# Layer 0 of a two-layer graph network: sums kept by node, two source tiles accumulated in PSUM, self product in the first pair

## The chip, the cores and the metric

The kernel runs on one core of a Trainium2 chip. The core has a matmul engine (PE, with its weight loads shown apart as PEld), VectorE (DVE), ScalarE (ACT), GpSimd (POOL) and a queue engine for DMAs (SP). They run side by side and wait for one another by semaphores. The metric is the device time of one execution in microseconds, the median of several runs.

## The reference

x has 3125 nodes of 128 features; 103125 edges go src to dst, sorted by dst, with a weight each. `ln` is layer norm without scale.

```python
h = maximum(ln(x), 0)
# layer 0: edge_index = (src, dst); sums go to row = src, features come from col = dst
x = x + relu(h @ W_S.T + b_S + segment_sum((h[dst] @ W_N.T + b_N) * exp(-edge_weight)[:, None], src))
h = maximum(ln(x), 0)
# layer 1: attention over incoming edges
q, k, v = h @ Wq + bq, h @ Wk + bk, h @ Wv + bv
logits = sum(q[dst] * k[src]) / sqrt(128)
x = x + elu(segment_sum(softmax_by_dst(logits) * v[src]) + h @ Ws + bs)
```

## The kernel before

Nodes come in 25 tiles of 128 (NT, the last partly empty). The kernel turns the edge list into dense 128 x 128 blocks: for each tile of dst nodes it counts, per pair of nodes, the edges (for layer 1, as logarithms stored to memory) and sums the edge weights (for layer 0).

The stretch that matters is the loop over the 25 dst tiles (L1160, `pe_tile`). A tile has two quads of 64 nodes, each with four groups (`pe_group`). For a quad DVE builds tables from the edges (`quad`, L880): the key table (L895), the low table (L898) and three weighted copies (L901), 128 elements wide per edge slot. PE multiplies them into PSUM (L1144, L1146), ACT moves counts (L605, into gst) and weight sums (L607, into wst) out. DVE builds a quad's tables once PE is through with the quad two before.

Layer 0's sum for dst tile s then goes like this. wst holds the tile's weights [dst node, src node]. PE turns it (L1107, 25 transposes of 128 x 128 in seven pieces: six of four blocks and one of one block, the list `PC`) into PSUM; ACT copies each piece to wsb (L589), a buffer of two pieces. PE multiplies it (L1117): the stationary operand is hvb, a copy of the tile's neighbour features (L582), the moving one the piece of up to 512 columns, and the product, features by nodes, goes into a PSUM bank. DVE adds it into kT (L838), which holds the sum with features on partitions. So each dst tile takes 7 products and 7 adds over all 3125 nodes. PE does the products of a tile during the next tile, DVE the adds during the tile after that. What a slot of PE holds: two groups, then up to two products, then up to two pieces to turn.

The self product (L1094, seven matmuls with W_S stationary) fills kT before the loop proper, during tiles 0 and 1, and ACT adds the bias while it copies (L569).

After the loop kT is turned back to nodes on partitions, five blocks at a time (`turn_sums`, L1124), DVE applies relu, adds x (L850) and takes the statistics of the second layer norm (L854, L858). The five rounds of projections follow (POOL normalises, PE turns, ACT copies with relu to hc, PE multiplies for k, v, q and skip, L1241 and L1246), and turn_sums of round d + 2 stands in round d. k and q share a pair of PSUM banks. Then come 25 tiles of attention (scores L1278, values L1288), which the change does not touch.

Order on every engine is the order of the code; only semaphores tie the engines. All engines meet at the end of a stage (`end_stage`, L176).

## Time and profile before

| | us |
|---|---|
| runs, median (lowest, highest) | 849.43 (847.42, 849.62) |
| profiled execution, time | 856.0 |
| profiled execution, span | 854.2 |
| PE busy | 755.5 (88%) |
| PE weight loads busy | 655.8 (77%) |
| DVE busy | 740.0 (87%) |
| ACT busy | 505.8 (59%) |
| POOL busy | 263.3 (31%) |

The span is from the first to the last instruction of the profiled execution. A busy matmul row runs to its modelled end, about 0.16 us beyond the start of the next one, so paces are read from start to start. The first layer's loop stands between 62 and 474 us of the span, the projections to 515, attention behind it.

### The profile page before, as it was taken

The page shows a single profiled execution, that of the slowest core. Times are in us where ns is not written, and L with a number is a line of the kernel's source. Part 1 is how long each engine was busy: PE and PEld are TensorE (multiplying, and loading weights), DVE is VectorE, ACT ScalarE, POOL GpSimd, SP SyncE. Part 2 cuts the span into 40 slices and gives each one's busy share as a digit, 9 for nine tenths or more (in the row PEclk, how much of TensorE's full clock was granted, in tenths as well). Part 3 has the DMA queues.
Part 4 walks back from the last instruction along what each step waited for, and adds up shares of the span by engine and source line. Part 5 has one row for each costly group of instructions (what it writes and reads, how often), then busy time and mean ns, then how long its engine had stood idle before and what let it go on. Part 6 is the DMA issues. An engine that isn't in the chain of part 4 may idle for free.

```text
span 854.2 us, 22930 instructions
## 1 busy us (share of the span) xinstructions
PE 755.5 (88%) x8801; PEld 655.8 (77%) x8848; DVE 740.0 (87%) x888; ACT 505.8 (59%) x1013; POOL 263.3 (31%) x205
## 2 busy tenths in 40 slices
PE   0258999999999999999999687899999999999996
PEld 0146777777777777777775466799999999999996
DVE  6776799999999999999994537899999999999982
ACT  4859766767677667676775251445456455445534
POOL 4634000000000000000000320556766766766766
PEclk9999999999999999999999798899999999999998
DMA  9821112313213123122131612203433433432400
GB/s 252 264 78 79 79 79 105 125 77 135 95 77 153 77 95 135 77 125 105 77 153 79 254 56 77 77 13 149 160 105 134 160 123 116 160 137 105 157 7 11
DMA packets 17661, 96.63 MB, mean 113 GB/s; under 512 B 2610, under 2 KB 8860, under 8 KB 11100
## 3 DMA queue, kind: packets, MB, share of 16 engines
q1 hardware_dynamic: 14572, 90.02, 27.8%
q0 software_dynamic: 3056, 6.17, 2.6%
q8 instruction: 21, 0.34, 0.2%
q14 instruction: 12, 0.10, 0.0%
HBM read 51.55 MB, written 44.63 MB: 113 GB/s over the span
## 4 chain that ended last, share of the span: by engine, by line
PE 70%; DVE 12%; issue 10%; ACT 5%; another core or an unknown queue 1%; DMA 1%; DVEq 1%; POOL 0%; POOLq 0%; ACTq 0%; PEldq 0%; PEld 0%
PE bank L1278 17%; PE bank L1288 16%; PE bank L1117 14%; PE bank L1107 5%; PE bank L1146 5%; DVE oh_key L901 5%; PE bank L1144 5%; DVE kT L838 3%; PE bank L1275 2%; PE bank L1241 2%; ACT kT L543 1%; PE bank L1246 1%; PE bank L1084 1%; DVE mx L1029 1%
## 5 line engine op out<-in xcount | busy, mean ns | idle before, releaser
L481 POOL TENSOR_TENSOR sm<-sm,mbc 128x896 f32<-128x896 f32 (+1 forms) x100 | 186.2, 1892 | 77.5 <-ACT mbc L703 77.5
L1117 PE MATMUL bank<-wsb,hvb 128*128 128x512 f32 (+1 forms) x350 | 165.2, 578 | 13.7 <-DVE kT L838 12.4
L1278 PE MATMUL bank<-qT,kT 128*128 (+1 forms) x1250 | 168.0, 279 | 6.9 <-issue 4.3
L1144 PE MATMUL bank<-oh_key,oh_lo 128*128 128x100 bf16 x1600 | 170.4, 208 | 1.9 <-ACT wst L607 1.9
L1146 PE MATMUL bank<-oh_key,oh_lo 128*128 128x50 bf16 x3200 | 170.8, 187 | 0.0
L1278 PEld LDWEIGHTS bank<-qT,kT 128*128 128x128 f32 x1250 | 163.8, 196 | 5.0 <-DVEq L178 1.2
L1146 PEld LDWEIGHTS bank<-oh_key,oh_lo 128*128 128x128 bf16 x3200 | 163.7, 97 | 1.1
L1144 PEld LDWEIGHTS bank<-oh_key,oh_lo 128*128 128x128 bf16 x1600 | 155.8, 97 | 7.7 <-issue 5.5
L589 ACT COPY wsb<-bank 128x512 f32<-128x512 f32 (+1 forms) x175 | 88.0, 552 | 106.4 <-PE bank L1107 106.4
L1288 PE MATMUL bank<-vals,sm 128*128 128x129 f32 x1250 | 148.5, 276 | 0.0
L1029 DVE TENSOR_REDUCE mx<-sm 128x128 f32<-128x3200 f32 x25 | 146.2, 5846 | 0.9
L707 ACT ACTIVATE sm<-sm 128x896 f32<-128x896 f32 (+1 forms) x100 | 86.8, 868 | 101.3 <-POOL sm L481 101.3
L1288 PEld LDWEIGHTS bank<-vals,sm 128*128 128x128 f32 x1250 | 144.7, 193 | 0.0
L901 DVE TENSOR_TENSOR oh_key<-oh_key,xt 128x1600 bf16<-128x1600 bf16 x150 | 141.9, 1002 | 0.0
L605 ACT ACTIVATE gst<-bank,tiny_col 128x400 f32<-128x400 f32 x200 | 122.8, 614 | 15.4 <-PE bank L1146 11.9
L465 POOL MEMSET vals<- 128x25 f32 x1 | 0.1, 142 | 401.8 <-PEq L178 401.8
L838 DVE TENSOR_TENSOR kT<-kT,bank 128x512 f32<-128x512 f32 (+1 forms) x175 | 105.6, 626 | 13.6 <-PE bank L1117 11.5
L983 DVE TENSOR_TENSOR sm<-bank,gl_sb 128x896 f32<-128x896 f32 (+1 forms) x100 | 98.6, 986 | 21.2 <-PE bank L1278 20.2
L898 DVE TENSOR_TENSOR oh_lo<-xt,lo_tab 128x4096 bf16<-128x4096 bf16 x50 | 114.2, 2284 | 0.0
L1107 PEld LDWEIGHTS bank<-ident,wst 128*128 128x128 f32 x625 | 82.0, 193 | 30.7 <-issue 30.0
L1117 PEld LDWEIGHTS bank<-wsb,hvb 128*128 128x128 f32 x350 | 56.4, 189 | 59.3 <-DVE kT L838 33.1
L607 ACT COPY wst<-bank 128x400 f32<-128x400 f32 x200 | 101.3, 506 | 0.0
(123 smaller groups left out, 697.9 us busy)
## 6 DMA issues: line engine op xcount, KB each, us to landing
gt<-gst SPq DMA_DIRECT2D x25, 1600.0 KB, 5.6
gl_sb<-gt SPq DMA_DIRECT2D x25, 1600.0 KB, 6.7
records<-rec SPq DMA_DIRECT2D x1, 2015.0 KB
out<-res SPq DMA_DIRECT2D x24, 64.0 KB, 1.6
src_i<-in_src SPq DMA_DIRECT2D x1, 403.0 KB, 6.5
w_in<-in_edge_weight SPq DMA_DIRECT2D x1, 403.0 KB, 6.9
dst_i<-in_dst SPq DMA_DIRECT2D x1, 403.0 KB, 7.4
dstn_i<-in_dst_next SPq DMA_DIRECT2D x1, 403.0 KB, 7.3
```

What stands on the lines that cost most here:

```text
L481: pool.tensor_tensor(part, part, mbc[:, v % 2:v % 2 + 1, :].to_broadcast([P, n, P]), ALU.subtract).then_inc(sub_done, 1)
L605: nc.scalar.activation(place, counts, ACT.Ln, bias=tiny_col[:, 0:1], scale=EULER).then_inc(evacs, 1)
L838: V.tensor_tensor(kT[:, cols], kT[:, cols], ps(6 + at)[:, 0:n * P], ALU.add).then_inc(l0_add, 1)
L898: V.tensor_tensor(oh_lo[:, u, :, :, :], along(F_LO, P), table(lo_tab, P), ALU.is_equal).then_inc(onehot, 1)
L901: V.tensor_tensor(block(1 + w), block(0), along(F_W + w, KEYS), ALU.mult).then_inc(onehot, 1)
L1029: V.tensor_reduce(mx[:], sm[:, v, :].rearrange("p (h d) -> p d h", d=P), AX, ALU.max).then_inc(mx_ready, 1)
L1107: ins = T.transpose(ps(4 + at)[:, h * P:(h + 1) * P], tile, ident[:])
L1117: T.matmul(ps(6 + at)[:, 0:n], hvb[:, w, :], wsb[:, at, 0:n], start=True, stop=True).then_inc(l0_mm, 1)
L1144: T.matmul(cells, lo, oh_key[:, u, m, 0:2 * KEYS, i], start=True, stop=False, skip_group_check=True)
L1146: ins = T.matmul(cells[:, KEYS:2 * KEYS], lo, oh_key[:, u, m, (1 + w) * KEYS:(2 + w) * KEYS, i], start=False, stop=w == 2, skip_group_chec ...
L1278: ins = T.matmul(score_bank(g)[:, j * P:(j + 1) * P], kT[:, (a + j) * P:(a + j + 1) * P], qT[:, bass.ds(t * P, P)], start=g < LIFT, stop=T ...
L1288: ins = T.matmul(ps(4 + v % 2)[:, 0:D + 1], sm[:, v, h * P:(h + 1) * P], vals[:, h, :], start=h == 0, stop=h == NT - 1)
```

## The change

The stationary operand of layer 0's products becomes the turned weights, 128 nodes at a time, and the moving one the neighbour features hv of the tile (128 columns), so the sum stands with nodes on partitions. `pe_sum` accumulates two dst tiles (a pair, 2p and 2p + 1) in PSUM before DVE adds the piece to kT once (`add_sum`). For the first pair the self product is accumulated in the same place, and DVE adds the bias, now a row (brow), instead of adding to kT. Both tiles' turned weights must be kept whole: wsb is now qT (free in this stage) for even tiles and wsb1 for odd ones. The copy hvb, the self products ahead of the loop, `turn_sums` and their semaphores are gone. Three tables say in which slot of a tile pieces are turned (TURNS), summed (SUMS) and added (ADDS, early and late place of each quad). Each table's first row is for even tiles, the second for odd ones. q's projection gets the bank pair that turn_sums used.

```diff
+
+
+TURNS = (((0, 1, 2), (3, 4), (5, 6), ()), ((0, 1), (2, 3), (4,), (5, 6)))
+SUMS = ((None, 0, 1, 2), (3, 4, 5, 6))
+ADDS = (((4, 5), (6, None)), ((0, 1), (2, 3)))
...
-        wsb = sb(s2, "wsb", [P, 2, 4 * P])
-        hvb = sb(s2, "hvb", [P, 2, D])
-        past_gl = sb(s2, "past_gl", [P, (P + KEYS) * (QN - TWO)], BF16)
+        wsb1 = sb(s2, "wsb1", [P, NP])
+        wsb = (qT, wsb1)
...
-            for i, b in enumerate((b_s, bq, bk)):
+            for i, b in enumerate((bq, bk)):
                 sp.dma_start(bcol[:, i:i + 1], b.rearrange("(p a) -> p a", a=1)).then_inc(s_wts, 16)
-            for i, b in enumerate((b_n, bv, b_skip)):
+            for i, b in enumerate((b_n, bv, b_skip, b_s)):
                 sp.dma_start(brow[:, i, :], b.rearrange("(a f) -> a f", a=1).to_broadcast([P, D])).then_inc(s_wts, 16)
...
-            def act_hv(s, w):
-
-                act.wait_ge(l0_mm, NPC * s + 1)
-                nc.scalar.copy(hvb[:, w, :], hv[:, bass.ds(s, 1), :].rearrange("p t f -> p (t f)")).then_inc(hvb_ready, 1)
-
-            def act_piece(s, w, j):
-                n = PC[j][1] * P
+            def act_piece(s, w, j, q):
+
+                a, n = PC[j][0], PC[j][1] * P
                 at = (w + j) % 2
                 act.wait_ge(turned, NPC + 1 + NPC * s + j + 1)
-                act.wait_ge(l0_mm, NPC * s + j + 1)
-                nc.scalar.copy(wsb[:, at, 0:n], ps(4 + at)[:, 0:n]).then_inc(l0_ev, 1)
+                act.wait_ge(l0_mm, NPC * (q + 1) + j + 1)
+                nc.scalar.copy(wsb[w][:, a * P:a * P + n], ps(4 + at)[:, 0:n]).then_inc(l0_ev, 1)
...
-                        if isinstance(t, int) and t == 1 and j == 1:
-                            act_self(4, NPC)
-                            act.wait_ge(s_hvb, len(TG))
-                        if before and j == 1:
-                            act_hv(t - 1, 1 - v)
-                        if before and j % 2 == 1:
-                            for piece in range(j - 1, min(j + 1, NPC)):
-                                act_piece(t - 1, 1 - v, piece)
+                        if p is not None and j % 2 == 1:
+                            for piece in TURNS[v][j // 2]:
+                                act_piece(t - 1, 1 - v, piece, p)
...
-                nc.scalar.activation(kT[:, cols], pair(2)[:, 0:CW], ACT.Identity, bias=bcol[:, 2:3]).then_inc(proj_a, 1)
+                nc.scalar.activation(kT[:, cols], pair(2)[:, 0:CW], ACT.Identity, bias=bcol[:, 1:2]).then_inc(proj_a, 1)
                 act.wait_ge(q_mm, d + 1)
-                nc.scalar.activation(qT[:, cols], pair(2)[:, 0:CW], ACT.Identity, bias=bcol[:, 3:4],
+                nc.scalar.activation(qT[:, cols], pair(0)[:, 0:CW], ACT.Identity, bias=bcol[:, 2:3],
                                      scale=float(D) ** -0.5).then_inc(proj_a, 1)
...
-            def dve_piece(s, w, j):
+            def add_sum(q, j, first=False):
 
                 a, n = PC[j]
-                at = (w + j) % 2
-                dve.wait_ge(l0_mm, 2 + NPC * s + j + 1)
-                dve.wait_ge(l0_add, NPC * s + j + 3)
-                cols = slice(a * P, (a + n) * P)
-                V.tensor_tensor(kT[:, cols], kT[:, cols], ps(6 + at)[:, 0:n * P], ALU.add).then_inc(l0_add, 1)
+                dve.wait_ge(l0_mm, 2 * NPC + NPC * q + j + 1)
+                part, rows = ps(6 + j % 2)[:, 0:n * P], kt3[:, a:a + n, :]
+                if first:
+                    V.tensor_tensor(rows, part.rearrange("p (t f) -> p t f", f=D),
+                                    brow[:, 3:4, :].to_broadcast([P, n, D]), ALU.add).then_inc(l0_add, 1)
+                else:
+                    dve.wait_ge(l0_add, 3 + NPC * q + j)
+                    flat = kT[:, a * P:(a + n) * P]
+                    V.tensor_tensor(flat, flat, part, ALU.add).then_inc(l0_add, 1)
...
-                dve.wait_ge(r_turned, d + 1)
-                V.scalar_tensor_tensor(out=flat, in0=pair(0)[:, 0:CW], scalar=0.0, in1=flat, op0=ALU.max,
+                V.scalar_tensor_tensor(out=flat, in0=kT[:, d * CW:(d + 1) * CW], scalar=0.0, in1=flat, op0=ALU.max,
...
                 for j in range(NPC):
-                    dve_piece(NT - 1, 0, j)
-                    if j == 2:
+                    add_sum(q, j)
+                    if j == 3:
+                        dve.wait_ge(l0_add, NPC + 2 + NPC * q + 2)
                         statistics(0)
...
+                    early, late = ADDS[v][u] if p is not None else (None, None)
+                    if early is not None:
+                        add_sum(p, early, first)
                     V.tensor_tensor(oh_lo[:, u, :, :, :], along(F_LO, P), table(lo_tab, P), ALU.is_equal).then_inc(onehot, 1)
+                    if late is not None:
+                        add_sum(p, late, first)
                     dve.wait_ge(onehot, (t * 2 + u) * HOTS + 1)
                     for w in range(3):
                         V.tensor_tensor(block(1 + w), block(0), along(F_W + w, KEYS), ALU.mult).then_inc(onehot, 1)
-                    for j in later:
-                        dve_piece(t - 2, v, j)
...
-                with dve.Fori(1, NT // 2) as i:
-                    dve_tile(i * 2, 0, True)
-                    dve_tile(i * 2 + 1, 1, True)
-                dve_tile(NT - 1, 0, True)
+                dve_tile(2, 0, None)
+                dve_tile(3, 1, 0, first=True)
+                dve_tile(4, 0, 0, first=True)
+                dve_tile(5, 1, 1)
+                with dve.Fori(3, NT // 2) as i:
+                    dve_tile(i * 2, 0, i - 2)
+                    dve_tile(i * 2 + 1, 1, i - 1)
+                dve_tile(NT - 1, 0, NT // 2 - 2)
                 for j in range(NPC):
-                    dve_piece(NT - 2, 1, j)
-                dve_last_tile()
+                    add_sum(NT // 2 - 1, j)
+                dve_last_tile(NT // 2)
...
-            def pe_self(from_, to):
-                pe.wait_ge(s_hnev, len(TG))
-                for j in range(from_, to):
-                    a, k = PC[j]
-                    if j >= 2:
-                        pe.wait_ge(acc_ev, j - 1)
-                    T.matmul(ps(6 + j % 2)[:, 0:k * P], wts[:, WS_, :], hT[:, a * P:(a + k) * P], start=True,
-                             stop=True).then_inc(acc_mm, 1)
...
-            def pe_product(s, w, j):
-                n = PC[j][1] * P
-                at = (w + j) % 2
-                if j == 0:
-                    pe.wait_ge(hvb_ready, s + 1)
-                pe.wait_ge(l0_ev, 2 + NPC * s + j + 1)
-                pe.wait_ge(l0_add, NPC + NPC * s + j + 1)
-                T.matmul(ps(6 + at)[:, 0:n], hvb[:, w, :], wsb[:, at, 0:n], start=True, stop=True).then_inc(l0_mm, 1)
-
-            def turn_sums(d):
-                if d >= 1:
-                    pe.wait_ge(ln_step, d * 3 - 2)
-                for j in range(HC):
-                    a = (d * HC + j) * P
-                    ins = T.transpose(pair(0)[:, j * P:(j + 1) * P], kT[:, a:a + P], ident[:])
-                ins.then_inc(r_turned, 1)
-
-            def pe_last(j):
-
-                if j == 4:
-                    pe.wait_ge(l0_add, NPC + 2 + NPC * (NT - 1) + 2)
-                    turn_sums(0)
+            def pe_sum(q, j, parts, first=False):
+
+                a, k = PC[j]
+                if first and j == 0:
+                    pe.wait_ge(s_hnev, len(TG))
+                    pe.wait_ge(s_hvb, len(TG))
+                pe.wait_ge(l0_add, NPC + 2 + NPC * q + max(j - 1, 0))
+                for s, w in parts:
+                    pe.wait_ge(l0_ev, 2 + NPC * s + j + 1)
+                for h in range(k):
+                    cols = slice((a + h) * P, (a + h + 1) * P)
+                    to = ps(6 + j % 2)[:, h * P:(h + 1) * P]
+                    if first:
+                        T.matmul(to, hT[:, cols], wts[:, WS_, :], start=True, stop=False, skip_group_check=True)
+                    for n, (s, w) in enumerate(parts):
+                        ins = T.matmul(to, wsb[w][:, cols], hv[:, bass.ds(s, 1), :].rearrange("p t f -> p (t f)"),
+                                       start=n == 0 and not first, stop=n == len(parts) - 1, skip_group_check=True)
+                ins.then_inc(l0_mm, 1)
...
                         if isinstance(t, int) and t == 0 and j == 6:
-                            pe_self(0, 4)
                             turn_windows(3, 5)
                         if isinstance(t, int) and t == 1 and j == 0:
-                            pe_self(4, NPC)
-                            pe.wait_ge(acc_ev, NPC)
                             pe.wait_ge(s_xtev, NB)
-                        if two_before and j == 0:
-                            pe_products(t - 2, v, SLOTS0)
+                        if p is not None and SUMS[v][j // 2] is not None:
+                            pe_pair(p, SUMS[v][j // 2], first)
                         if before:
-                            pe_products(t - 1, 1 - v, j)
-                            pe_turns(t - 1, 1 - v, j)
+                            pe_turns(t - 1, 1 - v, TURNS[v][j // 2])
...
-                pe_tile(0, 0, False, False)
-                pe_tile(1, 1, True, False)
-                with pe.Fori(1, NT // 2) as i:
-                    pe_tile(i * 2, 0, True, True)
-                    pe_tile(i * 2 + 1, 1, True, True)
-                pe_tile(NT - 1, 0, True, True)
-                pe_products(NT - 2, 1, SLOTS0)
-                for j in range(0, SLOTS0 + 2, 2):
-                    pe_products(NT - 1, 0, j)
-                    pe_turns(NT - 1, 0, j)
-                    pe_last(j)
+                pe_tile(0, 0, None, before=False)
+                pe_tile(1, 1, None)
+                pe_tile(2, 0, 0, first=True)
+                pe_tile(3, 1, 0, first=True)
+                with pe.Fori(2, NT // 2) as i:
+                    pe_tile(i * 2, 0, i - 1)
+                    pe_tile(i * 2 + 1, 1, i - 1)
+                pe_tile(NT - 1, 0, NT // 2 - 1)
+                for d in range(NG):
+                    pe_pair(NT // 2 - 1, SUMS[1][d])
+                    pe_turns(NT - 1, 0, TURNS[1][d])
+                for j in range(NPC):
+                    pe_sum(NT // 2, j, [(NT - 1, 0)])
...
-                if d + 2 < NC:
-                    turn_sums(d + 2)
                 pe.wait_ge(hc_ready, d + 1)
                 if d >= 1:
                     pe.wait_ge(proj_a, d * 2)
                     pe.wait_ge(proj_v, d * 2)
                 across(2, WK_, k_mm)
                 down(3, WV_, v_mm)
-                pe.wait_ge(proj_a, d * 2 + 1)
-                across(2, WQ_, q_mm)
+                across(0, WQ_, q_mm)
                 pe.wait_ge(proj_v, d * 2 + 1)
                 down(3, WX_, skip_mm)
```

On PE, in the loop, behind the two groups of the third slot of an even tile; hvb and wsb are the features and turned weights before, hv and qT or wsb1 those after. Before:

```order
L1115 REGISTER_ALU
L1116 REGISTER_ALU
L1117 MATMUL bank3<-wsb,hvb 128x512
L1115 REGISTER_ALU
L1116 REGISTER_ALU
L1117 MATMUL bank3<-wsb,hvb 128x512
L1107 MATMUL bank2<-ident,wst1 128x128 x8
```

After:

```order
L1102 REGISTER_ALU x2
L1109 MATMUL bank3<-hv,qT 128x128
L1109 MATMUL bank3<-hv,wsb1 128x128
L1109 MATMUL bank3<-hv,qT 128x128
L1109 MATMUL bank3<-hv,wsb1 128x128
L1109 MATMUL bank3<-hv,qT 128x128
L1109 MATMUL bank3<-hv,wsb1 128x128
L1109 MATMUL bank3<-hv,qT 128x128
L1109 MATMUL bank3<-hv,wsb1 128x128
L1085 REGISTER_ALU
L1091 MATMUL bank2<-ident,wst1 128x128 x4
```

Two wide products and two turned pieces stood in the slot. Now it holds one piece of a pair: eight matmuls of 128 columns, each with another stationary operand, and then the turned pieces.

On DVE, in the loop, the first quad of an even tile: the key table, the adds into kT, the low table. Before:

```order
L895 TENSOR_TENSOR oh_key<-xt,key_tab 128x16x100
L835 ISA
L838 TENSOR_TENSOR kT<-kT,bank3 128x512
L835 REGISTER_ALU
L838 TENSOR_TENSOR kT<-kT,bank3 128x512
L898 ISA
L898 TENSOR_TENSOR oh_lo<-xt,lo_tab 128x4096
```

After:

```order
L883 TENSOR_TENSOR oh_key<-xt,key_tab 128x16x100
L818 ISA
L824 REGISTER_ALU
L826 TENSOR_TENSOR kT<-kT,bank3 128x512
L887 ISA
L887 TENSOR_TENSOR oh_lo<-xt,lo_tab 128x4096
L818 REGISTER_ALU
L824 REGISTER_ALU
L826 TENSOR_TENSOR kT<-kT,bank3 128x512
```

Two adds stood between the two tables. Now there is one, and a second stands behind the low table, ahead of the weighted copies.

On ACT, in the loop, behind the first two groups of an even tile (the copies of turned pieces out of bank2). Before:

```order
L587 REGISTER_ALU
L589 COPY wsb<-bank2 128x512
L587 REGISTER_ALU
L588 REGISTER_ALU
L589 COPY wsb<-bank2 128x512
```

After:

```order
L580 REGISTER_ALU
L582 COPY wsb1<-bank2 128x512
L580 REGISTER_ALU
L582 COPY wsb1<-bank2 128x512
L580 REGISTER_ALU
L582 COPY wsb1<-bank2 128x512
```

Two pieces were copied there, now three.

## Rows read from the trace of the kernel before

**Rows 1.** Windows view, one tile of the first layer (busy us per engine, PEclk, DMA)
```profile
250.85:266.43 15.58, 15.14 (x237) 11.87 (x233) 15.50 (x18) 10.91 (x25) 0.00 (x0) 1.00 0.25 105
```

**Rows 2.** Timeline of PE, the tile from 257.04 (start us, us, engine, line)
```profile
257.04 0.21 PE L1144 MATMUL bank<-oh_key,oh_lo 128*128 128x100 bf16 x1
...
258.63 0.47 PE L1117 MATMUL bank<-wsb,hvb 128*128 128x128 f32 x2
...
262.97 1.13 PE L1117 MATMUL bank<-wsb,hvb 128*128 128x512 f32 x2 [0.44 <-DVE kT L838]
263.94 1.06 PE L1107 MATMUL bank<-ident,wst 128*128 128x128 f32 x8
...
266.43 1.96 PE L1117 MATMUL bank<-wsb,hvb 128*128 128x512 f32 x4
...
272.62 0.21 PE L1144 MATMUL bank<-oh_key,oh_lo 128*128 128x100 bf16 x1
```

**Rows 3.** Timeline of DVE in the same tile
```profile
262.83 0.99 DVE L895 TENSOR_TENSOR oh_key<-xt,key_tab 128x1600 bf16<-128x1600 bf16 x1
263.74 1.28 DVE L838 TENSOR_TENSOR kT<-kT,bank 128x512 f32<-128x512 f32 x2
264.93 2.29 DVE L898 TENSOR_TENSOR oh_lo<-xt,lo_tab 128x4096 bf16<-128x4096 bf16 x1
267.13 2.79 DVE L901 TENSOR_TENSOR oh_key<-oh_key,xt 128x1600 bf16<-128x1600 bf16 x3
269.84 1.28 DVE L838 TENSOR_TENSOR kT<-kT,bank 128x512 f32<-128x512 f32 x2
```

**Rows 4.** Timeline of ACT in the same tile
```profile
260.90 0.65 ACT L605 ACTIVATE gst<-bank,tiny_col 128x400 f32<-128x400 f32 x1
261.39 0.54 ACT L607 COPY wst<-bank 128x400 f32<-128x400 f32 x1
261.77 0.66 ACT L605 ACTIVATE gst<-bank,tiny_col 128x400 f32<-128x400 f32 x1
...
264.66 1.07 ACT L589 COPY wsb<-bank 128x512 f32<-128x512 f32 x2 [1.84 <-PE bank L1107]
```

**Rows 5.** Chain of waits in the attention layer (start us, us, what)
```profile
600.43 2.90 PE bank L1288 x26
```

**Rows 6.** Timeline of PE at the same place
```profile
603.17 2.83 PE L1278 MATMUL bank<-qT,kT 128*128 x22
```

**Rows 7.** Timeline of PE, first tiles, from three windows
```profile
76.73 3.87 PE L1094 MATMUL bank<-hT,wts 128*128 128x512 f32 x8
...
83.52 0.21 PE L1144 MATMUL bank<-oh_key,oh_lo 128*128 128x100 bf16 x1
...
101.20 0.21 PE L1144 MATMUL bank<-oh_key,oh_lo 128*128 128x100 bf16 x1
```

**Rows 8.** Timeline of DVE, the third tile's first table
```profile
91.04 0.99 DVE L895 TENSOR_TENSOR oh_key<-xt,key_tab 128x1600 bf16<-128x1600 bf16 x1 [8.21 <-PE bank L1146]
```

**Rows 9.** Timeline of PE: the last tile's first group, a late product
```profile
444.04 0.21 PE L1144 MATMUL bank<-oh_key,oh_lo 128*128 128x100 bf16 x1
...
471.59 1.10 PE L1117 MATMUL bank<-wsb,hvb 128*128 128x512 f32 x2 [2.30 <-DVE kT L838]
```

**Rows 10.** Timeline of DVE at the end of the first layer
```profile
468.47 0.82 DVE L850 SCALAR_TENSOR_TENSOR xs<-bank,xs 128x640 f32<-128x640 f32 x1 [1.61 <-PE bank L1124]
...
473.68 0.29 DVE L838 TENSOR_TENSOR kT<-kT,bank 128x128 f32<-128x128 f32 x1 [0.27 <-PE bank L1117]
```

**Rows 11.** Windows view, at the start of the projections
```profile
480.20:482.40 2.20, 2.13 (x10) 2.00 (x10) 0.85 (x8) 1.00 (x2) 0.85 (x2) 0.50 1.06 448
```

**Rows 12.** Chain of waits in the projections
```profile
482.67 1.89 PE bank L1241 x4
...
485.67 1.11 PE bank L1241 x4
```

**Rows 13.** Timeline of PE, second round of the projections
```profile
489.31 1.35 PE L1241 MATMUL bank<-hc,wts 128*128 128x512 f32 x4 [0.25 <-ACT hc L684]
```

More of the change, by code:

```diff
@@ L954, in _ @@
                     next_numbers(f_dnum, FD)
-                with dve.Fori(0, NT // 2) as i:
-                    for w in range(2):
-                        for j in range(NPC):
-                            dve_piece(i * 2 + w, w, j)
-                dve_last_tile()
+                for j in range(NPC):
+                    add_sum(0, j, first=True)
+                with dve.Fori(1, NT - 1) as s:
+                    for j in range(NPC):
+                        add_sum(s, j)
+                dve_last_tile(NT - 1)
             end_stage(dve, 2)
-            V.tensor_scalar(bcol[:, 3:4], bcol[:, 1:2], float(D) ** -0.5, None, ALU.mult).then_inc(s_qb, 1)
+            V.tensor_scalar(bcol[:, 2:3], bcol[:, 0:1], float(D) ** -0.5, None, ALU.mult).then_inc(s_qb, 1)
             inverse(0)
@@ L1148, in pe_group, with pe_pair, pe_turns, pe_tile @@
                     ins.then_inc(groups, 1)
-                def pe_products(s, w, j):
-                    for piece in range(max(j - 2, 0), min(j, NPC)):
-                        pe_product(s, w, piece)
-                def pe_turns(s, w, j):
-                    if j == 0:
-                        pe.wait_ge(evacs, 4 + (s + 1) * 2 * SLOTS0)
-                    for piece in range(j, min(j + 2, NPC)):
-                        pe_turn(s, w, piece, True)
-                def pe_tile(t, v, before, two_before):
+                def pe_pair(p, j, first=False):
+                    pe_sum(p, j, [(p * 2, 0), (p * 2 + 1, 1)], first)
+                def pe_turns(s, w, pieces):
+                    for j in pieces:
+                        if j == 0:
+                            pe.wait_ge(evacs, 4 + (s + 1) * 2 * SLOTS0)
+                        pe_turn(s, w, j, True)
+                def pe_tile(t, v, p, before=True, first=False):
                     for j in range(0, SLOTS0, 2):
@@ L1219, in _, with pe_tile_slow @@
                         pe.drain().then_inc(fs_mm, 1)
-                def pe_tile_slow(s, w, uses, last=False):
+                def pe_tile_slow(s, w, uses, first=False):
                     pe.wait_ge(fs_wl[w], uses * 16 + 16)
```

72 lines of the change are left out of this document (29 added, 43 removed).

## The prediction

> **What bounds the kernel now.** I read the page first (busy shares, chain), then the windows of the first layer, then one tile of it engine by engine in the timeline. The change touches only that layer and the projections behind it. In one tile of 15.58 us PE is busy 15.14 and DVE 15.50, at full granted clock [rows 1]; ACT has room. The reader is to see that two engines are full at once, and to ask which of them really works. PE's tile runs from 257.04 to 272.62 [rows 2]. Two groups of count matmuls take 1.59 (257.04 to 258.63), four such pairs a tile: 6.4. Eight transposes take 0.9 (the 1.06 of the row holds the last one's end), so 25 take 2.8. Two products of 512 columns take 1.80 (1.96 less the end), so the tile's 6.25 take 5.6 to 5.7. Sum 14.9; the remaining 0.7 is waiting, 0.44 of it for a DVE add into kT in the row at 262.97. DVE [rows 3]: key table 0.91 (262.83 to 263.74), two adds 1.19, low table 2.20, three weightings 2.71. Twice the tables is 11.6, seven adds (six full at 0.60, one of 0.19) are 3.8: 15.4 of 15.58. So DVE bounds the tile, and PE is only 0.7 behind it. That is the most that relieving DVE can give, per tile.
>
> **DVE.** Adds go from seven per tile to seven per two tiles: 175 become 91. DVE's work falls to 11.6 + 1.9 = 13.5 per tile. None of that shows by itself beyond PE's 14.9.
>
> **PE in the loop.** Per tile 7 products with 7 weights (512 columns) become 25 products with 25 weights (128 columns). The trace has the same form in the attention layer: fp32, new weights for each, 26 records in 2.90 [rows 5], 0.1117 us a record, two records per product (one of those streams 129 columns). 25 x 2 x 0.1117 = 5.6 per tile, what the wide ones took. So PE's work per pair of tiles is 12.8 groups + 5.6 transposes + 11.2 sums = 29.5, and 0.1 for the starts of pieces. The bound on the other side is the neighbouring row, 22 records in 2.83 [rows 6], 0.129 each, end and a halt between groups included. I take 0.1117 since the sums stand 16 records in a row with no halt inside.
>
> **New waits in the loop.** (1) In an even tile three pieces are turned in one go behind the first two groups, with two PSUM buffers. The third needs ACT's copy of the first. Count from the groups' start: groups end 1.59; ACT begins on the second group about 0.25 later (ACT takes up a turned piece at 264.66, where the first four of the transposes from 263.94 are issued by 264.39 [rows 2, 4]), and its two moves take 0.49 and 0.38 (260.90, 261.39, 261.77 [rows 4]), but the first group's moves hold it, so it is free at 2.8. Copy 0.54 and 0.12 to pass it on: 3.45. PE has done two pieces at 2.49. It waits 0.96. (2) DVE's fifth piece. Count from the end of the even tile's fourth group: PE runs sum 0, turn, two groups, sum 1, turn and so on, and ends sum 5 at 21.9, the pair's last turn at 24.9. DVE may add piece 5 only then: 22.14 to 22.74, the three weightings to 25.45, and PE starts the next even tile at 25.57 instead of 24.93: 0.64. The waits that DVE itself gets (1.5 for piece 1, 1.5 for piece 5) lie in its spare time otherwise. Pair: 29.6 + 0.96 + 0.64 = 31.2, against 2 x 15.58 = 31.16. Ten pairs: **+0.5**. The loop changes its bound, not its length.
>
> **Start.** The self product was 3.7 (76.73 to 80.43, from the row's 3.87) and 3.0 more behind tile 1's first groups. It goes, so tile 1 begins at 79.8 instead of 83.52 [rows 7]. Tile 1 then needs 6.4 + 2.8 of PE and 1.1 of waits, ending at 90.1. DVE's table for tile 2 can start once tile 1's first four groups are done (two pairs of groups and a turn between, 1.59 + 0.90 + 1.59) and 0.25 passed, at 84.1 instead of 91.04 [rows 8]; with 5.8 of tables and no adds tile 2 starts at 90.1 instead of 101.20: -11.1. But tiles 2 and 3 now carry the self products too: 25 x 2 x 0.1117 = 5.6 on 29.5, with 1.3 of waits 36.4 against 31.16: +5.2. **Start: -5.9.**
>
> **End.** Before, from the last tile's first group (444.04 [rows 9]) to the last add (473.68 + 0.29 [rows 10]) 29.9. After, PE lags further: the last tile (6.4 groups, 5.4 sums, 2.8 transposes, 0.96 wait) 15.5, then sums 3 to 6 of the pair 5.8, transposes 2.8, the single tile's sums 5.6, about 2.0 for an add standing behind the statistics (the same wait is 2.30 now [rows 9], where the statistics begin at 468.47 [rows 10]), the last add 0.5: 32.2. **End: +2.3.**
>
> **Projections.** Five transposes per round (turn_sums) go, and q gets a bank of its own. The rounds do not shorten: the key product waits for ACT's relu copy, which hangs on the transpose before, not on turn_sums (wait of 0.25 left at 489.31 [rows 13]), and each copy out of the shared bank is over when v's product ends. What may be lost is clock: PE is at 0.50, the lower level of 1.2 GHz, with 10 records of transposes under way [rows 11], and its first key product takes 1.89 where a later one takes 1.11 [rows 12]. Without turn_sums PE does less before the rise. Bounds: nothing, or v and q of the first round at half clock too, 2 x 1.1 = +2.2. I take **+1.0**, between.
> The Trainium skill (TensorE: Matmul & The Clock Gate, Part 4: PE-mode transpose) says that a transpose does not count as PE activity for the clock as other matmuls do. By that, taking transposes away delays nothing, and this term is 0; by the row alone it stays open.
>
> **Sum.** -5.9 + 0.5 + 2.3 + 1.0 = -2.1. The profiled execution took 856.0 (span 854.2), the median shown is 849.43; the change of 2.1 on either gives 853.9 and **847.3**. Nothing in the attention layer moves.
>
> **Rivals.**
> A (forecast): loop bound moves from DVE to PE at equal length; 847.3, own range 843 to 851.
> B, faster: the two new waits don't arise or half close, because ACT and DVE pass work on sooner than my 0.25 and 0.12. For it: each depends on under 1 us. Against: the copy stands behind four moves of ACT whatever the latency. Price: 1.6 x 12 = 19 if both go (828), the DVE one alone 0.64 x 12 = 8: 840.
> C, slower: short fp32 products with their own weights, register addresses and three semaphore checks per piece don't reach 0.1117. Place: each sum piece on PE. 1250 records in the layer, so each ns costs 1.25 us; from 0.1155 a record the kernel is slower by over 0.3%. At 0.120, half way to rows 6, +10.4: 858; at 0.129 +21.6: 868. For it: rows 6; against: rows 5, and the same layer's transposes at 0.113.
> D, slower: the jump back at PE's loop end costs a fetch, since its body grows by 72 matmul records and their weight loads. Before, tile 272.62 starts without a gap [rows 2]. If 3 us came at each of 10 rounds: 877.
> For D the Trainium skill (Runtime: NRT & Kernel Launch, Instruction fetch mechanics) says that PE's instruction store holds 2048 instructions and that a jump out of the held part stalls; by that number both bodies fit, and D adds 0.
> That the change does not do what it says (adds not halved) has no room: the count of adds is fixed by the code.
>
> **Chances.** A 0.48, B 0.25, C 0.24, D 0.03. A change of 0.3% (2.5 us) is about what can be told from none. A splits 0.40 faster, 0.50 same, 0.10 slower; B nearly all faster; C mostly slower, 0.20 of it same. Faster 0.19 + 0.24 = 0.43, same 0.24 + 0.01 + 0.06 = 0.31, slower 0.05 + 0.18 + 0.03 = 0.26. The range reaches to B's nearer price and to C's nearer one: 839 to 858.
>
> **What would show it.** DVE's busy share in the loop falls to about 13.5 of 15.6, PE's stays near 15; a pair of tiles lasts 31.2; 16 records of a sum take 1.79 to 1.82; the third turned piece waits 0.96 for ACT and the even tile's first group 0.64 for DVE's weighting; tile 2 starts near 90, tile 4 near 126.5; the layer ends near 471 instead of 474. A pair under 30.5 or sums over 1.85 would prove it wrong, and so would a gap at the loop's jump.

## The result and the profile after

The changed kernel took 854.18 us (median; 852.44 to 855.72), the kernel before 849.43 in the same comparison: 1.0051 times as long, 95% interval 1.0033 to 1.0068, that is +4.2 to +4.8. In a second comparison the same two kernels stood at 860.39 and 856.16: 1.0049 [1.0029, 1.0068]. The forecast was 847.3, 0.25% faster. The time lies in the range of 839 to 858, but the sign is wrong.

The level moved by 6.7 us from one comparison to the next for the kernel before itself. A row shows where such a step can come from: ahead of the layer, the profiled execution of before holds for 6.56 us (41.24, "another core or an unknown queue" in its chain), the one of after doesn't, and the repetition of after has 7.17 at 40.36. So kernels are compared here by their ratio to the kernel before in the same comparison, and traces from the layer's first group of count matmuls on.

The page of the changed kernel, profiled execution (span 852.8, 854.67 in all):

```profile
PE 760.9 (89%) x9759; PEld 735.2 (86%) x9759; DVE 698.9 (82%) x804; ACT 498.9 (59%) x981; POOL 267.2 (31%) x205
...
PE 78%; DVE 8%; ACT 6%; issue 5%; DMA 1%; POOL 0%; DVEq 0%; PEld 0%; ACTq 0%; POOLq 0%; PEldq 0%
```

DVE's 740.0 became 698.9, as wanted, but PE rose from 755.5 to 760.9 and its share of the chain from 70% to 78%. The bound has moved to PE.

Timeline of PE after the change: the first groups of tiles 1, 2 and 4, then the pair of tiles from 249.00, then the last tile (start us, us, engine, line; in brackets the wait ahead and who ended it). It answers to [rows 2, 7, 9]:

```profile
74.38 0.21 PE L1124 MATMUL bank<-oh_key,oh_lo 128*128 128x100 bf16 x1
84.78 0.22 PE L1124 MATMUL bank<-oh_key,oh_lo 128*128 128x100 bf16 x1 [0.32 <-DVE oh_key L892]
121.91 0.22 PE L1124 MATMUL bank<-oh_key,oh_lo 128*128 128x100 bf16 x1 [0.23 <-DVE oh_key L892]
...
249.00 0.22 PE L1124 MATMUL bank<-oh_key,oh_lo 128*128 128x100 bf16 x1 [0.54 <-DVE oh_key L892]
250.61 1.15 PE L1091 MATMUL bank<-ident,wst 128*128 128x128 f32 x8
252.41 0.72 PE L1091 MATMUL bank<-ident,wst 128*128 128x128 f32 x4 [0.65 <-ACT wsb L582]
254.56 0.47 PE L1109 MATMUL bank<-hv,qT 128*128 x2
254.86 0.39 PE L1109 MATMUL bank<-hv,wsb 128*128 x2
264.78 0.21 PE L1124 MATMUL bank<-oh_key,oh_lo 128*128 128x100 bf16 x1
280.78 0.22 PE L1124 MATMUL bank<-oh_key,oh_lo 128*128 128x100 bf16 x1 [0.54 <-DVE oh_key L892]
...
439.46 0.22 PE L1124 MATMUL bank<-oh_key,oh_lo 128*128 128x100 bf16 x1 [0.37 <-DVE oh_key L892]
```

A pair of tiles lasts 280.78 - 249.00 = 31.78, over all ten (439.46 - 121.91) / 10 = 31.75; before it was 31.17. Both forecast waits are there and in their places: the third turned piece waits for ACT, the even tile's first group for DVE's weighting. From the starts of the rows around them the second costs 0.71. In the first PE stands still for 0.82, and the first transpose behind it takes 0.10 more than the others, 0.9 together.

The pair of rows at 254.56 and 254.86 holds what the forecast lacks. Each has two records, but the second begins 0.30 after the first, and from then on one follows the other each 0.22 (2 x 0.1117): the first fp32 product behind the bf16 groups costs 0.08 more. So a sum of 16 records takes 1.87. In the tail of the layer the same kernel has a sum that stands behind transposes, and it takes 1.78, from 457.91 to 459.69:

```profile
457.91 0.39 PE L1109 MATMUL bank<-hv,qT 128*128 128x128 f32 x2
...
459.69 1.06 PE L1091 MATMUL bank<-ident,wst 128*128 128x128 f32 x8
```

The rows of weight loads (PEld) show what goes with it. The load of a sum's first record starts 0.03 ahead of its product (254.53, 254.56), that of the third 0.11 ahead (254.75, 254.86). Behind the wait for ACT load and transpose start together (252.41):

```profile
252.41 0.41 PEld L1091 LDWEIGHTS bank<-ident,wst 128*128 128x128 f32 x3 [0.84 <-ACT wsb L582]
...
254.53 0.30 PEld L1109 LDWEIGHTS bank<-hv,qT 128*128 128x128 f32 x2
254.75 0.30 PEld L1109 LDWEIGHTS bank<-hv,wsb 128*128 128x128 f32 x2
```

The lead that is missing, 0.08 and 0.11, is about the extra, 0.08 and 0.10. So the fp32 weight load that nothing covers may be the cause, rather than the change of type. No run separates the two.

DVE at the end of the layer, and PE's wait there, answering to [rows 9, 10]:

```profile
468.45 0.82 DVE L837 SCALAR_TENSOR_TENSOR xs<-kT,xs 128x640 f32<-128x640 f32 x1
...
470.76 1.52 DVE L826 TENSOR_TENSOR kT<-kT,bank 128x512 f32<-128x512 f32 x3
```

```profile
471.47 0.49 PE L1109 MATMUL bank<-hv,qT 128*128 128x128 f32 x2 [1.73 <-DVE kT L826]
```

The last sum waits 1.73 for an add that stands behind the statistics, and the last add ends at 472.28.

Where the time went, stage by stage. The second pair of traces is the repetition of both kernels:

| stage | forecast | first pair of traces | second pair |
|---|---|---|---|
| start: first group to tile 4 | -5.9 | 66.96 - 70.14 = -3.2 | 66.96 - 70.11 = -3.2 |
| ten pairs of tiles | +0.5 | 317.55 - 311.67 = +5.9 | 317.49 - 311.67 = +5.8 |
| end: last tile to last add | +2.3 | 32.82 - 29.93 = +2.9 | 32.83 - 30.25 = +2.6 |
| projections | +1.0 | 43.31 - 41.50 = +1.8 | 43.46 - 40.60 = +2.9 |
| sum of these | -2.1 | +7.4 | +8.1 |
| attention to the end | 0 | -1.5 | -1.2 |
| ahead of the first group | 0 | -7.3 (the hold) | -0.8 |

The spans differ by the last three rows together, -1.4 and +6.1. The medians say +4.2 to +4.8; each trace is one execution, and the second pair comes from two comparisons. The attention's 1.2 to 1.5 is not laid to the change: the same attention code took 335.7 to 339.3 us in the traces of all kernels here. The loop alone is as large as the whole loss.

### The profile page after: what moved, and what is told of

It reads as the page before. It is cut to its first block, busy times and chain, and to the rows that moved or that the text cites. A ratio compares the mean times of both kernels' runs of the same rounds, so it can differ in the third digit from the quotient of the medians.

```text
span 852.8 us, 24429 instructions
## 1 busy us (share of the span) xinstructions
PE 760.9 (89%) x9759; PEld 735.2 (86%) x9759; DVE 698.9 (82%) x804; ACT 498.9 (59%) x981; POOL 267.2 (31%) x205
## 4 chain that ended last, share of the span: by engine, by line
PE 78%; DVE 8%; ACT 6%; issue 5%; DMA 1%; POOL 0%; DVEq 0%; PEld 0%; ACTq 0%; POOLq 0%; PEldq 0%
PE bank L1109 16%; PE bank L1259 16%; PE bank L1249 16%; PE bank L1126 8%; PE bank L1124 7%; PE bank L1091 6%; DVE oh_key L892 3%; PE bank L1246 3%; PE bank L1215 2%; PE bank L1220 1%; ACT kT L547 1%; PE bank L1077 1%; ACT wsb L582 1%; DVE mx L1022 1%; DVE junk L732 1%
## 5 line engine op out<-in xcount | busy, mean ns | idle before, releaser
L598 ACT ACTIVATE gst<-bank,tiny_col 128x400 f32<-128x400 f32 x200 | 121.0, 605 | 37.8 <-PE bank L1126 32.4
L1109 PE MATMUL bank<-hv,qT 128*128 (+1 forms) x650 | 128.3, 285 | 1.7 <-DVE kT L826 1.7
L1109 PE MATMUL bank<-hv,wsb 128*128 (+1 forms) x600 | 116.0, 275 | 0.0
L826 DVE TENSOR_TENSOR kT<-kT,bank 128x512 f32<-128x512 f32 (+1 forms) x84 | 52.7, 628 | 58.2 <-PE bank L1109 57.7
L600 ACT COPY wst<-bank 128x400 f32<-128x400 f32 x200 | 99.3, 496 | 0.0
L1109 PEld LDWEIGHTS bank<-hv,qT 128*128 128x128 f32 x650 | 96.7, 191 | 2.1 <-DVE kT L826 1.9
L1091 PE MATMUL bank<-ident,wst 128*128 128x128 f32 x625 | 88.8, 279 | 7.9 <-ACT wsb L582 7.9
```

Of the source, the lines that this page charges most:

```text
L598: nc.scalar.activation(place, counts, ACT.Ln, bias=tiny_col[:, 0:1], scale=EULER).then_inc(evacs, 1)
L600: nc.scalar.copy(sums, cells[:, :, KEYS:2 * KEYS]).then_inc(evacs, 1)
L1091: ins = T.transpose(ps(4 + at)[:, h * P:(h + 1) * P], tile, ident[:])
L1109: ins = T.matmul(to, wsb[w][:, cols], hv[:, bass.ds(s, 1), :].rearrange("p t f -> p (t f)"), start=n == 0 and not first, stop=n == len(par ...
```

## The experiments

**The two waits.** Only the tables of orders are edited. The first kernel changes TURNS, the second ADDS, the third both.

```
-TURNS = (((0, 1, 2), (3, 4), (5, 6), ()), ((0, 1), (2, 3), (4,), (5, 6)))
+TURNS = (((0, 1), (2, 3), (4, 5), (6,)), ((0, 1), (2, 3), (4,), (5, 6)))     first, third
-ADDS = (((4, 5), (6, None)), ((0, 1), (2, 3)))
+ADDS = (((4, None), (5, 6)), ((0, 1), (2, 3)))                               second, third
```

Turns alone: 

> The even tile turns two, two, two and one piece behind its four pairs of groups, not three, two, two and none. Theory (the pair of tiles lost 0.6 us to two waits and to 8 switches from bf16 groups to fp32 products at 0.08 us each, and each wait is worth its own length): the wait of the third turned piece for ACT (0.82 of a pair's 31.78) goes, PE is at work in its place, ten pairs of the loop fall by about 8 us, the first and last tiles by 1.5: 844.5 against 854.2. The sums stay at 1.865 us for 16 records and the wait for DVE's weighting at 0.7 a pair. Rival (the loop is held by something else, such as DVE's chain over the adds): the wait moves to another piece and the time stays within 1 us of 854.2.

Adds alone: 

> DVE adds pieces 5 and 6 of the pair in the even tile's second half, piece 4 in its first, so that no add stands between PE's sum 5 and the weighting of the next even tile. Theory: the wait of the even tile's first group for DVE's weighting (0.71 a pair) goes, 0.6 to 0.7 a pair, about 6 to 7 us in the loop: 847.5. Rival (the weighting is late because DVE itself is behind, or PE's sums then wait for the later adds to free their PSUM bank): a wait of the same size shows at a sum's first record, and the time stays at 854.

Both: 

> Both edits of the two kernels above. Theory (the waits are separate and add up): 1.5 a pair, a pair of 30.3, about 16 to 17 us in all: 837.5. What is left of a pair is 12.8 of groups, 11.7 of sums, 5.8 of transposes. Rival (one cover for the other: when one wait goes, the other grows): no better than the better of the two alone, 844 to 847.

Measured against before: turns 0.9917 [0.9893, 0.994], adds 0.9954 [0.9933, 0.9976], both 0.9825 [0.9801, 0.9848]. The changed kernel stands at 1.0049 in its repetition, so the edits are worth 1.3%, 0.9% and 2.2% (11, 8 and 19 us). The expected times were on the level of the first comparison; as shares of the changed kernel's time they were 0.989, 0.992 and 0.980, and 0.987, 0.991 and 0.978 came out. The pairs of tiles lasted 30.85, 31.05 and 30.15: less by 0.90, 0.71 and 1.61, and 0.90 + 0.71 is 1.61. The theory holds and both gains add up; the rivals (a wait that moves elsewhere, one wait that covers for the other) are excluded. PE in the kernel with both orders, a pair of tiles from 247.97 to 278.12, with no wait ahead of any first group, and the window of this pair (columns as in [rows 1]), where PE is busy all 30.15:

```profile
247.97 0.21 PE L1124 MATMUL bank<-oh_key,oh_lo 128*128 128x100 bf16 x1
...
262.83 0.21 PE L1124 MATMUL bank<-oh_key,oh_lo 128*128 128x100 bf16 x1
...
278.12 0.21 PE L1124 MATMUL bank<-oh_key,oh_lo 128*128 128x100 bf16 x1
```

```profile
247.97:278.12 30.15, 30.15 (x537) 30.06 (x535) 27.48 (x28) 21.59 (x47) 0.00 (x0) 1.00 0.26 109
```

**Wide products, tiles still paired.** hv becomes the weights again, and 512 columns of the turned sums stream. With it come back ACT's copy of hv into a fixed buffer, the bias by partition, and the transposes of the sums in the projections.

```
-                for h in range(k):                      # 128 columns, own weights each
-                        ins = T.matmul(to, wsb[w][:, cols], hv[:, bass.ds(s, 1), :]...)
+                cols = slice(a * P, (a + k) * P)        # up to 512 columns
+                    ins = T.matmul(to, hvb[:, w, :], wsb[w][:, cols], ...)
+                            act_hv(p, t - 2, 0, 2)      # in ACT's even tile, behind group 2
```

> Only the accumulation of two tiles in PSUM is kept; the products turn back to the wide form (hv of the tile as weights, 512 columns of the turned sums moving, features on the partitions), with the copy of hv by ACT, the bias by partition and the transposes of the sums ahead of the statistics. Orders and waits in the loop stay as after the change. Theory (the narrow form costs 0.8937 per 512 columns at 0.1117 a record where the wide one costs 0.86 at 0.43 a record, and both pay 0.08 when they follow bf16 groups): a sum falls from 1.865 to 1.80, 0.4 a pair, 4 to 5 us in the layer, and the projections' clock comes back with the transposes (1.5): about 848.5. The two waits stay at 0.7 to 0.8. Rival (the forecast's pricing: narrow and wide cost the same, the loss is in the waits alone): a sum at 1.86 in both, only the clock's 1.5 comes back: 852.5. Rival (the narrow form is the whole loss, as 25 weight loads per tile are not hidden): the pair of tiles falls below 31.0, total below 846.

It took 1.0128 [1.0106, 1.0149], slower than both kernels, which no expectation had. The pair lasted 32.41. One row says why, and it is a fault of the experiment: the copy of hv stood too late on ACT, and the first sum of each pair waited for it.

```profile
264.50 1.12 PE L1121 MATMUL bank<-qT,hvb 128*128 128x512 f32 x2 [0.87 <-ACT hvb L590]
```

Counted from the starts of the rows, the wait costs 1.05. Less that, the pair is 31.36, 0.39 under the changed kernel, and the sum itself is the 1.80 expected. A sum of 1.86 or a pair under 31.0, as the two rivals had it, did not come. A second version has both forecast waits removed and the copy ahead of the even tile's first evacuation:

> The wide form again, with both orders changed, and with ACT's copy of hv ahead of the even tile's first evacuation (the first wide kernel made PE wait 0.87 a pair for it). Theory: a sum 1.80 instead of 1.865 and the last one as before, 0.39 a pair less than the version with both orders (30.15): 29.8; start -0.5, projections' clock -1.5: 6 us under it, ratio 0.9755. Rival (the copy of hv by ACT and the longer records bring other waits of the same size): pair 30.1, ratio 0.981.

It took 0.9759 [0.9738, 0.978], pair 29.74, 0.41 under the 30.15 of the narrow form: both as expected. That the total fits is partly luck. Against the trace of the version with both orders the projections gave 0.4 instead of 1.5, and 1.6 came from tile 0, where the clock did not fall (see the start below). Two sums of it on PE, 256.79 to 258.60 and 260.29 to 262.10:

```profile
256.79 1.10 PE L1121 MATMUL bank<-qT,hvb 128*128 128x512 f32 x2
257.73 1.02 PE L1121 MATMUL bank<-wsb,hvb 128*128 128x512 f32 x2
...
260.29 1.10 PE L1121 MATMUL bank<-qT,hvb 128*128 128x512 f32 x2
261.23 1.02 PE L1121 MATMUL bank<-wsb,hvb 128*128 128x512 f32 x2
```

So the narrow form costs 0.4 a pair, 4 us in the loop, and the two waits 1.61. Two tiles per addition with the wide form are worth 31.17 - 29.74 = 1.43 a pair against the kernel before. By its ratio this is the fastest version that was run: 2.4% under the kernel before, 2.9% under the change.

**The price of going from bf16 to fp32.** Two kernels on the version with both orders. In the one the turned pieces stand between a slot's two groups (in the loop only), in the other ahead of its sum.

```
                         pe_group(t, j)
+                        if before and not isinstance(t, int): pe_turns(...)    # split
                         pe_group(t, j + 1)
+                        if before: pe_turns(t - 1, 1 - v, TURNS[v][j // 2])    # order: ahead of the sum
                         if p is not None and SUMS[v][j // 2] is not None: pe_pair(...)
-                        if before: pe_turns(t - 1, 1 - v, TURNS[v][j // 2])
```

Split: 

> On the version with both orders changed (pair 30.15): in the loop the turned pieces stand between the two groups of a slot, the sum behind the second, so PE goes 8 more times a pair from bf16 groups to fp32 records (one of the sum-less slot is there already: 7 more). Theory (each such turn of form costs 0.08 us, wherever it stands): 0.56 a pair more, 30.7, about +6 us of the total over the 0.9825 ratio: 0.989. Sums stay at 1.865. Rival (the 0.08 belongs to the sum's own start: its register address and three waits): transposes behind a group cost no more than behind a sum, the pair stays at 30.15, ratio 0.982.

Order: 

> On the version with both orders changed: the turned pieces of a slot stand ahead of its sum. The number of changes from bf16 to fp32 stays. Theory (the cost is of the first fp32 record behind bf16 groups): 16 records of a sum fall from 1.865 to 1.785 where pieces are turned ahead of them, the first transpose takes 0.19 instead of 0.11, the pair stays at 30.15 within 0.15. Rival (cost of the sum's own start): sums stay at 1.865, transposes at 0.1125.

Split took 1.0079 [1.0048, 1.0109], pair 32.29, far more than the 30.7 expected. Its PE rows show two things. New waits of the pieces for ACT, in the even tile, make up some 1.3 of the 2.1 a pair:

```profile
255.12 1.17 PE L1091 MATMUL bank<-ident,wst 128*128 128x128 f32 x8 [0.23 <-ACT qT L582]
258.65 1.21 PE L1091 MATMUL bank<-ident,wst 128*128 128x128 f32 x8 [0.75 <-ACT wsb L582]
```

And in the odd tile, which has none (270.61 to 286.26, 15.65 against 15.29), four more turns of form cost 0.36, 0.09 each. The size per turn was about right (0.08 expected), the total missed what the split does to ACT. Order took 0.9864 [0.9838, 0.989], pair 30.48. The row of its eight transposes behind groups, and the first two of the sum behind them:

```profile
252.01 1.15 PE L1091 MATMUL bank<-ident,wst 128*128 128x128 f32 x8
252.99 0.39 PE L1109 MATMUL bank<-hv,qT 128*128 x2
253.22 0.39 PE L1109 MATMUL bank<-hv,wsb 128*128 x2
254.78 0.21 PE L1124 MATMUL bank<-oh_key,oh_lo 128*128 128x100 bf16 x1
```

The sum is 254.78 - 252.99 = 1.79 instead of 1.865 and its first product has lost the extra, while the eight transposes ahead take 0.98 instead of 0.90 (254.00 to 254.90 in the version with both orders). The extra goes with the place behind the groups, not with the sum's address or its waits: that rival is excluded. Here the kernel was not within 0.15 of its base but 0.33 slower a pair, 0.26 of it a wait ahead of the odd tile's first group (the sum ends at 262.72, the group starts at 262.98), for which the trace names no releaser.

**Repetitions.** The changed kernel and the kernel before, each with a trace of its own:

> The changed kernel once more, beside the kernel before on this chip, since the kernel before took 856.2 in the last comparison and 849.4 in the first. Theory (the layer's loop alone is worth +5.9, the whole +4 to +5, whatever the level of the chip or of a start that waits longer for the windows): ratio 1.004 to 1.007, a pair of tiles of 31.75 to 31.78. Rival (part of the 0.5% was the one hold of 6.6 us ahead of the layer, present in one kernel and not in the other): ratio off by up to 0.008 either way with the same pair.

> The kernel before once more with a profile, for three readings that rest on one trace of it: the hold of 6.56 us ahead of the layer, the place at which the clock rises in the first projection round (v 1.28 there, 1.5 to 2.3 in the kernels after), and the 21 halts of 0.2 us in the attention layer's score matmuls, which no trace of the changed kernels shows. Theory for the clock (it scatters in the same code): v's ten records at 1.5 or more here too. Rival (the stage before has the earlier rise): 1.28 again. Halts: if they come again they belong to the kernel before and are worth 1.5 us to the change; if not, they were that one execution's. The pair of tiles stays at 31.17, ratio 1.000 within its interval.

The changed kernel came out at 1.0049 with a pair of 31.75, so the loss doesn't hang on the hold, which this trace has. The kernel before has the hold again (6.83 at 40.87) and gave 0.9981 [0.9961, 1.0001] against itself, pair 31.17. The halts of 0.2 us in the attention layer are absent (1.0 us of idle ahead of L1278 instead of 6.9), so they were of one execution. The rise of the clock came early again, v 1.28: the theory that it merely scatters failed, the rival held.

**The clock in the projections.** On the version with both orders:

```
+            def idle_turns():
+                for j in range(HC):
+                    T.transpose(pair(0)[:, CW:CW + P], wts[:, WS_, :], ident[:])
```

> The version with both orders changed, a second time, as the base that the two kernels of this comparison are read against and for the place in the first projection round at which the clock rises in a second trace. Ratio 0.980 to 0.985, pair 30.15; the clock rises in v's products (1.7 to 1.8 instead of 1.28) or as late as q's: the traces so far show 1.73 to 2.34 for v in the same code.

> On the version with both orders changed: five transposes whose result nothing reads stand at three places where the transposes of the sums stood before the change (behind the last tile's fourth sum, ahead of the first projection round, and behind that round's transposes of xn). Theory (PE's work ahead of the projections, transposes included, brings the rise of the clock forward, as the forecast's middle value had it): v's ten records at 1.28 to 1.5, q's four at 1.25, 0.5 to 1.5 us less, ratio 0.979 to 0.982. Rival (transposes do not bring the rise forward; what the traces show is scatter): v at 1.7 to 2.3 again, ratio within 0.001 of the base or up to 1 us more for the transposes themselves.

The ratio was 0.983 [0.9788, 0.9872] with the idle transposes, 0.9824 [0.9782, 0.9866] without. v's ten records took 1.48 with them, 1.54 and 1.73 in the two traces without (1.7 or more was expected of the second one, which gave 1.54). The 1.48 lies in the theory's range, the time in the rival's, and 1.48 against 1.54 is less than the scatter of the same code. So no effect of the transposes is seen, in one trace of them. That agrees with the forecast's other reading, by the Trainium skill (TensorE: Matmul & The Clock Gate, Part 4: PE-mode transpose): a transpose does not count as PE activity for the clock as other matmuls do. The two wide versions, which have the transposes of the sums again, point the same way: v took 1.50 and 1.78. But the kernel before rises earlier in both its traces, so something else of its stage matters. Its first round in the repetition:

```profile
481.43 1.72 PE L1241 MATMUL bank<-hc,wts 128*128 128x512 f32 x4
482.99 1.28 PE L1246 MATMUL bank<-wts,hc 128*128 128x128 f32 x10
484.11 1.28 PE L1241 MATMUL bank<-hc,wts 128*128 128x512 f32 x4
```

and the same three products (k, v, q) after the change:

```profile
481.18 2.50 PE L1215 MATMUL bank<-hc,wts 128*128 128x512 f32 x4 [0.85 <-ACT hc L668]
483.47 2.34 PE L1220 MATMUL bank<-wts,hc 128*128 128x128 f32 x10
485.60 1.45 PE L1215 MATMUL bank<-hc,wts 128*128 128x512 f32 x4
```

The granted clock is 0.50 until about 486 after the change; in the kernel before it rises inside k. Counted from the layer's last add, it rises after 8.8 and 10.1 us in the kernel before, and after 11.4 to 15.4 in the twelve traces of the changed kernel and its variants. There v took 1.48 to 1.78 in six and 2.34 in six, never 1.28, with or without transposes.

**The self product.** Left out of the version with both orders, so its output lacks x times W_s:

```
-                    if first:
-                        T.matmul(to, hT[:, cols], wts[:, WS_, :], start=True, stop=False, ...)
```

> On the version with both orders changed: the self product (x times W_s) is left out, 25 fp32 products of two records in tiles 2 and 3. Theory (they cost their 5.6 us one for one, since PE bounds these tiles): tile 2 to tile 4 takes 30.3 to 30.7 instead of 35.75, 5.0 to 5.4 us less, ratio 0.976 to 0.9765. Rival (DVE's tables bound tiles 2 and 3, which are still filling): 33 or more, ratio 0.980.

It took 0.9778 [0.9736, 0.9821]. From tile 2 to tile 4 it is 30.16 instead of 35.75: 5.6, one for one. The theory holds and the rival (DVE bounds these tiles) doesn't. But the total fell by less, 0.46% or 3.9 us. In the trace, against its base, tile 0 is 1.5 shorter, and the projections are 3.3 and the attention 3.3 longer. Of the projections 1.7 are a round in which the clock dropped once more:

```profile
471.50:473.50 2.00, 1.45 (x2) 0.68 (x3) 1.51 (x10) 0.49 (x1) 1.92 (x2) 0.69 0.03 8
473.50:475.50 2.00, 2.00 (x10) 1.75 (x9) 0.00 (x0) 0.79 (x1) 0.43 (x1) 0.50 0.00 0
```

(windows: length, busy PE, PEld, DVE, ACT, POOL, granted clock, DMA share, GB/s). The split version has such a round too (7.76 long like this one, 6.10 in the other traces), so it does not come from leaving the self product out.

## Why the prediction was wrong

**The bound and the rivals' mechanisms.** "The loop changes its bound, not its length" was right in its first half. DVE's relief does not show by itself, and both new waits are there (1.61 a pair, forecast 1.60), so rival B fails. There is no gap at the loop's jump (rival D): with both orders changed every pair starts without a wait.

**The step that failed: in "PE in the loop" the term "0.1 for the starts of pieces", where the runs show 8 x 0.08 = 0.64 a pair.** The pace was right, 0.1117 inside a sum. What was left out is the first product behind the groups, in 7 of the 8 slots of a pair, and the first transpose in the eighth. The wide products of before were priced with it: 1.80 for four records holds it once (4 x 0.43 + 0.08). The narrow ones, "what the wide ones took", were priced without. By measured terms the pair is 12.74 groups + 11.17 products + 5.59 transposes + 8 x 0.08 + 1.61 waits = 31.75, and without the waits 30.14, which is the 30.15 of the version with both orders. The forecast's 31.2 lacks 0.55, all of it in these starts. (Its own terms 12.8 + 5.6 + 11.2 make 29.6, not 29.5; by the measured terms 29.5 is right.)

The number stood in the rows that were used: in [rows 2] the two narrow records at 258.63, behind the groups, take 0.47, where the eight transposes take 1.06, of which 0.90 is eight paces and 0.16 the end. Two paces and that end are 0.39; 0.08 is left over.

In the kernel before, PE had 29.76 of work a pair and stood waiting for 1.40; after, 30.14 and 1.61. The ten pairs make the +5.9 measured against +0.5: 3.8 of work, which the narrow form brought, and 2.1 of waits.

**Rival C** named the right place, the sums, with the wrong cause. 1.865 for 16 records is 0.1166 each, above its point of decision at 0.1155, yet no record is slow except the first. The forecast's own sign of being wrong, "sums over 1.85", came. (In the chances 0.20 of C's 0.24 is 0.05, where the sum takes 0.06; nothing hangs on it.)

**Start, -5.9 forecast, -3.2 measured.** Tile 1 behaved as worked out (10.4 long, 17.7 before). Tile 0 gave 1.86 instead of 3.7. In the changed kernel's trace PE's granted clock falls to 0.50 for 3.4 us there, and in the version with turns alone it doesn't. The windows of both from 6 to 8 us behind the first group, the changed kernel first:

```profile
60.95:62.95 2.00, 2.00 (x12) 2.00 (x12) 2.00 (x2) 1.10 (x3) 0.92 (x1) 0.55 0.00 0
```

```profile
67.45:69.45 2.00, 2.00 (x22) 1.81 (x21) 2.00 (x2) 1.69 (x5) 1.10 (x1) 1.00 0.00 0
```

Twelve records against 22 in two microseconds. The step from tile 0 to tile 1 is 19.4 to 19.5 in six traces of kernels with the change and 17.9 in six, whatever the edit, so this is 1.5 us that comes and goes. Neither trace of the kernel before has such a fall; whether the change makes it possible stays open. The remaining 0.3 is the transposes of the windows, which wait 1.06 for ACT, against 0.78 behind the self product before. Tiles 2 and 3 took 37.13, not 36.4: 0.64 of it are their eight starts behind groups.

**End, +2.3 forecast, +2.9 and +2.6 measured.** Four starts behind groups in the last tile account for 0.32. The last sums with their wait for the statistics (1.73, and 1.89 from start to start) and the last add took 8.4, forecast 8.1.

**Projections, +1.0 forecast, +1.8 and +2.9 measured.** From k's start to the next round's it is 8.33 against 6.85 in the first pair and 8.31 against 6.48 in the second. So k, v and q of the first round lose 1.5 and 1.8 to the clock, inside the bounds given (0 to +2.2). The rest, 0.4 and 1.1, lies between the last add and k's start and is not explained. For the cause named, turn_sums, nothing speaks: put back, the transposes bring no early rise. What makes the clock rise sooner in the kernel before stays open. A term of 0, the other reading, was wrong too.

In the first pair of traces the miss of 6.9 us is 5.4 in the loop, 2.7 at the start, 0.6 at the end and 0.8 in the projections, less the attention's 1.5 and 1.1 of differences between executions. That the time lies in the range is luck: the upper end was set by rival C, whose cause is not what happened.

## What to carry to other kernels

Before a form of matmul is priced from rows of another stage, look at what stands ahead of it there and here: the first fp32 product behind short bf16 ones has a price of its own, and each interleaving pays it. The idea of adding once for two tiles was sound: with wide products it took 29.74 a pair for 31.17, by the 1.40 of waits that the kernel before had. When relief on one engine moves the bound to another, the orders written for the old bound are the next thing to change. Here two table entries, worth 1.6 us a pair, turned +0.5% into -1.8%, and a forecast that names two waits and their sizes has already written that experiment.

## What the hardware showed beyond the forecast

- The first fp32 record behind the bf16 groups costs 0.08 us more, be it a narrow product (0.193 instead of 0.112), a wide one (0.51 instead of 0.43) or a transpose (0.193 instead of 0.113). The first behind a wait for another engine costs 0.10 more (0.213).
- The same code in the same place had the clock at 0.50 for 3.4 us or at 1.00 in tile 0, worth 1.5 us, in six traces each. In the 3.4 us ahead of it PE was busy for 1.77 in the changed kernel, where the clock fell, and for 1.77 in the version with turns alone, where it didn't. In the projections it rose from 0.50 at points some us apart. Totals scatter by that much.
- A hold of 6.5 to 7.3 us ahead of the layer, in two traces in two parts, is in ten of the fourteen. The four without it belong to comparisons in which the kernel before took 849.4 and 851.1, the others, but for the trace of before itself (856.0), to comparisons in which it took 856.2 and 857.3.
